# Weight casts of a fused attention and mixture-of-experts kernel moved to VectorE, and its attention weights staged through one buffer

## The chip, the cores and the metric

The kernel runs on the 8 cores of one Trainium2 chip. Each core computes two of the 16 sequences by itself; the cores exchange nothing. The time is that of the slowest core, in microseconds of device time. The trace is that of one profiled execution, on the slowest of its cores.

## The reference

```python
x = x + _layernorm(_attn(_layernorm(x), Wq, bq, Wk, bk, Wv, bv))   # out = einsum('bqk,bqd->bkd', softmax(q k / 32), v)
x = x + _layernorm(_ffn(_layernorm(x), gate_w, w1, w2, w3, ws1, ws2, ws3))

# _ffn, for all tokens t and experts e:
weights, indices = _gate(xt, gate_w)      # softmax over 16 experts, best 2 of 4 groups, best 4 experts
c = c.at[arange(T)[:, None], indices].add(weights)
h1 = einsum('td,edi->tei', xt, w1)
h3 = einsum('td,edi->tei', xt, w3)
y = einsum('tei,eid,te->td', silu(h1) * h3, w2, c)
z = silu(xt @ ws1) * (xt @ ws3) @ ws2
```

x is 16 sequences of 2048 tokens with 1024 features, all in float32. An expert's w1 and w3 are 1024x512, its w2 is 512x1024; ws1, ws2, ws3 are 1024x1024.

## The kernel before

A core works through its two sequences ("batches", b = 0 and 1) one after the other. Every expert is computed for every token, and its result is multiplied by the token's gate weight (zero for most). The shared expert is cut into two more of the same shape, so there are NPE = 18 units for each chunk of 512 tokens, four chunks (g = 0 to 3) a batch, and 72 units a batch.

The program is written by hand as five queues, one for each engine: "t" TensorE (PE in the profile), "v" VectorE (DVE), "s" ScalarE (ACT), "g" GpSimd (POOL) and "d" SyncE (SP), which issues all DMAs. `pr.on(engine, function)` appends a function to a queue, and each engine works through its queue in the order in which the functions were appended. `mark` and `wait` are semaphores between them. All engine instructions go through one helper, so the profile puts them on line 33, all DMAs on line 61 and the waits on line 57; they are told apart by tiles and shapes.

Each batch has these stages:

- *Attention weights* (lines 325 to 382). Wq, Wk, Wv come in two halves of 2 MB each (`h0`, `h1`), both issued at once into `wstA`, a part of the large buffer `RA`. DVE casts each half to bf16 into `Wbf` (128x4096 a cast), then PE transposes it and ACT copies the result to `RW`. The next weight's halves are issued after the cast of both, and its first cast waits for the transposes. Then PE spreads the bias row bv over the partitions, and ACT copies that to `bvrep` (lines 384 to 403).
- *Projections* (lines 405 to 516), from x loaded in tiles of 128 tokens (`a1_d`) and normalized by `emit_ln`, whose square root runs on ACT; then scores, softmax and the attention output, which leaves x1 in DRAM (`x1park`).
- *Router* (`back_kb`, `gate_group`) for the four tiles of a chunk: layernorm, transposes, the gate's logits, and a long row of small DVE operations that picks the experts.
- *Units* (lines 1143 to 1157). For unit u PE does h1(u) (32 matmuls of 128x512), y(u-1) (4 column groups `q_` of 8 matmuls) and h3(u) (32). ACT does four silu, DVE four multiplications `amul` of silu(h1) with h3 into `apb`, which y reads, and four accumulations `stt` of y into `Ysb`, which is `RA`. y uses two pairs of PSUM banks in turn: its third and fourth column groups wait for the first and second accumulation of the same unit (line 1014). The accumulations of unit u-1 stand on DVE ahead of the multiplications of unit u.
- *Final layernorm and output* (`fin_tile`), a chunk behind; POOL adds the residual (`outadd`), and SP sends the tile out. The last store of a batch waits on SP for POOL's addition.

In batch 0, chunk 0 (`conv` in `unit_dma`) the expert weights come as float32, in six pieces of 1 MB a unit (pieces 0 and 1: w1, 2 and 3: w3, 4 and 5: w2). They land in turn in the two halves of the staging buffer `wstF` (a part of `RV`); piece k+2 is sent when piece k has been cast. ACT casts pieces 0, 2, 3 and 4, POOL 1 and 5, into the unit's weight buffers. Two stores, `tee` (2 MB, after the casts of pieces 0 to 3) and `tee2` (1 MB, after 4 and 5), keep the bf16 weights in DRAM (`wbf16`), from which the other 126 units load them. The stores stand in SP's queue behind the unit's loads and ahead of the next unit's.

Of the kernel before, what the change touches and what calls it, by code (L numbers as in the profile page):

```python
# [12 lines left out]
P = 128  # L13
# [3 lines left out]
NEXP = 16  # L17
# [48 lines left out]
class Prog:  # L66
# [14 lines left out]
    def mget(self, key):  # L81
        return self.M.get(key)

    def mput(self, key, mark):
        self.M[key] = mark
# [22 lines left out]
def build(S, marks_in, stop=99):  # L108
    NB = 2
    TT = S // P  # L110
# [27 lines left out]
    with contextlib.ExitStack() as ctx:  # L138
# [15 lines left out]
        RA = ent(nc.sbuf_tensor("RA", [P, 16384], F32))  # L154
        RQ = ent(nc.sbuf_tensor("RQ", [P, 16384], BF16))
        RK = ent(nc.sbuf_tensor("RK", [P, 8192], F32))
        RV = ent(nc.sbuf_tensor("RV", [P, 8192], F32))
# [13 lines left out]
        pr = Prog(block, sems, dsems, marks_in)  # L171
        mget, mput = pr.mget, pr.mput
# [5 lines left out]

        RAb = RA[:].bitcast(BF16)
        Wbf = RAb[:, 0:8192]  # L180
        wstA = RA[:, 4096:12288]
        brow = RA[0:1, 12288:15360]
        gwsv = RA[0:NEXP, 15360:16384]
        xstage = RA[:, 4096:6144]
        xnbf = RAb[:, 12288:14336]
        sqA1 = RA[:, 7168:9216]
# [27 lines left out]
        def bankb(i, w=1):  # L214
            return PS[:, i * 512:(i + w) * 512].bitcast(BF16)
# [99 lines left out]
        try:  # L315
            for b in range(NB):
# [8 lines left out]
                for wi, (Wsrc, WTdst) in enumerate([(Wq, WTq), (Wk, WTk), (Wv, WTv)]):  # L325
                    key = f"b{b}w{wi}"

                    def a0_d(q, Wsrc=Wsrc, key=key, wi=wi, b=b):
                        if wi > 0:
                            q.wait(mget(f"b{b}w{wi - 1}cast"))  # L330
                        elif b > 0:
                            q.wait(mget(f"b{b - 1}ffn_cast_s"))
                            q.wait(mget(f"b{b - 1}ffn_cast_g"))
                        mput(key + "h0", q.dma(
                            wstA[:, 0:4096].rearrange("p (a d) -> p a d", a=4),
                            Wsrc[0:512, :].rearrange("(a p) d -> p a d", p=P),
                            pr.ds("wA")))
                        mput(key + "h1", q.dma(
                            wstA[:, 4096:8192].rearrange("p (a d) -> p a d", a=4),
                            Wsrc[512:1024, :].rearrange("(a p) d -> p a d", p=P),  # L340
                            pr.ds("wB")))
                    pr.on("d", a0_d)

                    def a0_v(v, key=key, wi=wi, b=b):
                        if wi > 0:
                            v.wait(mget(f"b{b}w{wi - 1}tr"))
                        elif b > 0:
                            v.wait(mget(f"b{b - 1}fin_done"))
                        v.wait(mget(key + "h0"))
                        v.tensor_copy(Wbf[:, 0:4096], wstA[:, 0:4096])  # L350
                        v.wait(mget(key + "h1"))
                        v.tensor_copy(Wbf[:, 4096:8192], wstA[:, 4096:8192])
                        mput(key + "cast", v.mark())
                    pr.on("v", a0_v)

                    def a0_t(t, key=key, wi=wi, b=b):
                        t.wait(mget(key + "cast"))
                        if b == 0 and wi == 0:
                            t.wait(mget("s_bias"))
                        if b > 0 and wi == 0:  # L360
                            t.wait(mget(f"b{b - 1}fin_done"))
                        for dt in range(DS):
                            pb = 6 + dt % 2
                            if dt >= 2:
                                t.wait(mget(key + f"tre{dt - 2}"))
                            elif wi > 0:
                                t.wait(mget(f"b{b}w{wi - 1}tre{dt + 6}"))
                            for a in range(DS):
                                t.transpose(bankb(pb)[:, a * P:(a + 1) * P],
                                            Wbf[:, a * 1024 + dt * P: a * 1024 + dt * P + P],  # L370
                                            identb[:])
                            mput(key + f"tr{dt}", t.mark())
                        mput(key + "tr", t.mark())
                    pr.on("t", a0_t)

                    def a0_s(s, key=key, WTdst=WTdst):
                        for dt in range(DS):
                            pb = 6 + dt % 2
                            s.wait(mget(key + f"tr{dt}"))
                            s.copy(WTdst[:, dt * 1024:(dt + 1) * 1024], bankb(pb)[:, 0:1024])  # L380
                            mput(key + f"tre{dt}", s.mark())
                    pr.on("s", a0_s)
# [22 lines left out]
                for cc in range(NCH):  # L405
                    gcc = b * NCH + cc

                    def a1_d(q, b=b, cc=cc, gcc=gcc):
                        if cc == 0:
                            q.wait(mget(f"b{b}w2cast"))  # L410
                        for ti in range(4):
                            gt = cc * 4 + ti
                            gti = b * TT + gt
                            q.wait(mget(f"T{gti - 2}ln"))
                            mput(f"T{gti}x",
                                 q.dma(xstage[:, (gti % 2) * D:(gti % 2 + 1) * D],
                                       x_in[b, gt * P:(gt + 1) * P, :],
                                       pr.ds("xA" if gti % 2 == 0 else "xB")))
                    pr.on("d", a1_d)

                    for ti in range(4):
# [503 lines left out]
                def cast_body(x, u, piece, b=b):  # L925
                    gslot = (u * 6 + piece) % 2
                    par = u % 2
                    x.wait(mget(f"b{b}U{u}p{piece}dma"))
                    if u >= 2:
                        x.wait(mget(f"T{u - 2}tee1" if piece < 4 else f"T{u - 2}tee2"))  # L930
                    if u >= 2:
                        if piece < 2:
                            x.wait(mget(f"b{b}U{u - 2}h1"))
                        elif piece < 4:
                            x.wait(mget(f"b{b}U{u - 2}h3"))
                        else:
                            x.wait(mget(f"b{b}U{u - 2}y3"))
                    else:
                        x.wait(mget(f"g{b * NCH + NCH - 1}qkvmm"))
                        if b > 0:  # L940
                            x.wait(mget(f"b{b - 1}ffn_mm_done"))
                    if piece < 2:
                        col, dstb = piece * 2048, wbufs[par]
                    elif piece < 4:
                        col, dstb = 4096 + (piece - 2) * 2048, wbufs[par]
                    else:
                        col, dstb = (piece - 4) * 2048, w2bufs[par]
                    if isinstance(x.e, bass.BassScalarEngine):
                        x.copy(dstb[:, col:col + 2048],
                               wstF[:, gslot * 2048:(gslot + 1) * 2048])  # L950
                    else:
                        x.tensor_copy(dstb[:, col:col + 2048],
                                      wstF[:, gslot * 2048:(gslot + 1) * 2048])
                    mput(f"b{b}U{u}p{piece}cast", x.mark())

                def unit_casts(u, b=b):
                    def uc_s(s, u=u):
                        for piece in (0, 2, 3, 4):
                            cast_body(s, u, piece)
                    pr.on("s", uc_s)  # L960

                    def uc_g(g_, u=u):
                        for piece in (1, 5):
                            cast_body(g_, u, piece)
                    pr.on("g", uc_g)

                def unit_h1(t, u, b=b):
                    g, e = u // NPE, u % NPE
# [165 lines left out]
                for g in range(NCH):  # L1134
# [8 lines left out]
                    for e in range(NPE):  # L1143
                        u = g * NPE + e
# [91 lines left out]
```

How the kernel before makes its waits and increments, by code:

```python
    def mark(self):  # L45
        if not self._marked:
            self._last.then_inc(self.sem, 1)
            self.n += 1
            self._marked = True
        return (self.sem, self.n)
# [1 line left out]
    def wait(self, mark):  # L52
        if mark is None:
            return
        sem, n = mark
        if n > 0:
            self.e.wait_ge(sem, n)
# [1 line left out]
    def dma(self, out, in_, s):  # L59
        sem, counts, key = s
        self.e.dma_start(out=out, in_=in_).then_inc(sem, 16)
        counts[key] += 16
        return (sem, counts[key])
# [1137 lines left out]
        def final_d(raw):  # L1201
            for k, n in finals.items():
                if n > 0:
                    raw.wait_ge(dsems[k], n)
```

## Time and profile before

| | |
|---|---|
| runs | 5165.06 us median of 3 (lowest 5155.02) |
| profiled execution | 5155.31 us, span 5153.7 us (core 1; the others 5138.4 to 5153.4) |
| granted clock, mean of the span | 0.881 to 0.884 on all cores |
| PE busy | 4145.2 us (80%) |
| DVE busy | 1956.8 us (38%) |
| ACT busy | 890.9 us (17%) |
| POOL busy | 154.7 us (3%) |
| DMA | 695.6 MB, mean 135 GB/s |

The busy shares are those of the whole span, over stages with different limits. PEclk is the granted clock as a share of 2.4 GHz. In the rows, `RV<-w` is a load of a float32 piece of an expert's weights, `wbf<-RW` a store of bf16 weights, `RW<-wbf` a load of them; a bracket gives the idle time of the engine before the group and what ended it.

### The profile page before, as it was taken

How to read it: one execution, taken by the hardware profiler on the slowest of the kernel's cores; microseconds unless marked ns; L12 is line 12 of the kernel's file. 1: busy time of each engine (PE TensorE's matmuls, PEld its weight loads, DVE VectorE, ACT ScalarE, POOL GpSimd, SP SyncE). 2: the span in 40 equal slices, each digit the busy share in tenths (PEclk: the TensorE clock that was granted, in tenths of full speed). 3: DMA queues.
4: the chain of work that ended last, by engine and by line, in shares of the span. 5: the costliest groups of instructions: out<-in, count | busy, mean ns of one | idle time of the engine just before them, and what ended most of it. 6: DMA issues, size and time to landing. Idle time of an engine off the chain costs nothing.

```text
span 5153.7 us, 53876 instructions; the slowest of 8 cores (5138.4 to 5153.7 us)
## 1 busy us (share of the span) xinstructions
PE 4145.2 (80%) x18864; PEld 1933.0 (38%) x18864; DVE 1956.8 (38%) x2996; ACT 890.9 (17%) x1350; POOL 154.7 (3%) x78
## 2 busy tenths in 40 slices
PE   4679757666899699879945679799979969996995
PEld 2234323222444344334423234344444434443442
DVE  2323532223433533443352333443343343344335
ACT  2124122222111111111102123111111111111110
POOL 0000001111000000000010000000000000000001
PEclk8789878888799799979976789899989979997997
DMA  3100478888344334334433101434334433433443
GB/s 123 33 9 13 137 234 277 275 275 266 131 157 153 108 138 153 120 130 159 150 101 120 33 9 37 159 123 150 128 123 156 149 121 138 149 119 128 154 153 108
DMA packets 123563, 695.61 MB, mean 135 GB/s; under 512 B 9620, under 2 KB 9620, under 8 KB 86440
## 3 DMA queue, kind: packets, MB, share of 16 engines
q1 hardware_dynamic: 123304, 692.18, 38.7%
q8 instruction: 160, 2.62, 0.2%
q14 instruction: 99, 0.81, 0.1%
HBM read 601.96 MB, written 90.18 MB: 134 GB/s over the span
## 4 chain that ended last, share of the span: by engine, by line
PE 67%; DMA 14%; DVE 9%; issue 4%; ACT 3%; POOL 2%; SPq 1%; DVEq 1%; POOLq 0%; ACTq 0%
PE PS L33 67%; DMA RV<-w 7%; DVE st L33 2%; DMA RK<-x 2%; DVE RK L33 2%; DVE RA L33 2%; DMA RV<-x1park 1%; POOL RW L33 1%; POOL RV L33 1%; DVE c_buf L33 1%; DVE glog L33 1%; DVE RV L33 1%; ACT RK L33 1%; ACT RW L33 1%; DMA RA<-Wv 1%
## 5 line engine op out<-in xcount | busy, mean ns | idle before, releaser
L33 PE MATMUL PS<-RQ,RW 128*128 128x512 bf16 x9216 | 2091.1, 389 | 275.7 <-POOL RW L33 183.9
L33 PEld LDWEIGHTS PS<-RQ,RW 128*128 128x128 bf16 x9216 | 917.9, 100 | 1424.8 <-issue 389.0
L33 PE MATMUL PS<-RW,RK 128*128 128x512 bf16 x4608 | 1036.4, 382 | 155.0 <-DVE RA L33 144.3
L33 DVE SCALAR_TENSOR_TENSOR RA<-PS,c_buf,RA 128x1024 f32<-128x1024 f32 x480 | 616.2, 1284 | 1319.2 <-PE PS L33 1318.7
L33 ACT ACTIVATE RK<-PS 128x512 f32<-128x512 f32 (+1 forms) x608 | 370.7, 620 | 2360.5 <-PE PS L33 2346.8
L33 PEld LDWEIGHTS PS<-RW,RK 128*128 128x128 bf16 x4608 | 433.8, 98 | 735.4 <-issue 265.6
L33 DVE TENSOR_TENSOR RK<-RK,PS 128x512 bf16<-128x512 f32 x576 | 394.0, 687 | 491.3 <-PE PS L33 491.1
L33 PE MATMUL PS<-identb,RA 128*128 128x128 bf16 x640 | 74.5, 295 | 309.8 <-DVE RA L33 299.0
L33 PE MATMUL PS<-RV,RA 128*128 128x512 bf16 x1024 | 228.4, 383 | 28.7 <-DVE RK L33 15.1
L33 PE MATMUL PS<-RA,RW 128*128 128x512 bf16 x1024 | 239.1, 398 | 8.5 <-DVE RA L33 8.5
L33 PE MATMUL PS<-RK,RQ 128*128 128x512 bf16 x1024 | 221.3, 379 | 3.0 <-DVE RV L33 3.0
L33 ACT CAST RW<-RV 128x2048 bf16<-128x2048 f32 x72 | 136.6, 1898 | 429.8 <-DMA RV<-w 367.2
L33 POOL TENSOR_TENSOR RV<-RV 128x1024 f32<-128x1024 f32 x32 | 85.3, 2667 | 3794.6 <-DMA RV<-x1park 2321.2
L33 PEld LDWEIGHTS PS<-identb,RA 128*128 128x128 bf16 x640 | 59.4, 133 | 328.5 <-issue 326.5
L33 PE MATMUL PS<-identf,RK 128*128 128x128 f32 x256 | 62.1, 424 | 138.1 <-DVE RK L33 138.1
L33 DVE TENSOR_TENSOR RV<-PS,RA 128x1024 bf16<-128x1024 f32 x32 | 39.2, 1224 | 323.2 <-PE PS L33 323.2
L33 PEld LDWEIGHTS PS<-RV,RA 128*128 128x128 bf16 x1024 | 99.1, 98 | 157.9 <-issue 45.6
L33 PEld LDWEIGHTS PS<-RA,RW 128*128 128x128 bf16 x1024 | 103.5, 102 | 142.3 <-issue 33.1
L33 PE MATMUL PS<-gwT,RK 128*128 128x16 f32 x512 | 114.2, 373 | 46.8 <-ACT RK L33 46.8
L33 PEld LDWEIGHTS PS<-RK,RQ 128*128 128x128 bf16 x1024 | 100.1, 98 | 124.2 <-issue 3.9
L33 PEld LDWEIGHTS PS<-gwT,RK 128*128 128x128 f32 x512 | 111.7, 331 | 58.7 <-issue 58.7
L33 ACT ACTIVATE st<-st 128x1 f32<-128x1 f32 x128 | 26.0, 203 | 621.3 <-DVE st L33 621.2
(73 smaller groups left out, 1597.7 us busy)
## 6 DMA issues: line engine op xcount, KB each, us to landing
RW<-wbf SPq DMA_DIRECT2D x126, 2048.0 KB, 7.8
RW<-wbf SPq DMA_DIRECT2D x126, 1024.0 KB, 4.8
RV<-w SPq DMA_DIRECT2D x96, 1024.0 KB, 7.6
wbf<-RW SPq DMA_DIRECT2D x18, 2048.0 KB, 14.6
wbf<-RW SPq DMA_DIRECT2D x18, 1024.0 KB, 7.7
RA<-x SPq DMA_DIRECT2D x32, 512.0 KB, 3.3
RK<-x SPq DMA_DIRECT2D x32, 512.0 KB, 4.5
x1park<-RK SPq DMA_DIRECT2D x32, 512.0 KB, 3.0
```

What stands on the lines that cost most here:

```text
L33: self._last = getattr(self.e, name)(*a, **k)
```

## The change

Three things are changed.

- The cast of pieces 1, 3 and 5 of each converted unit is done by DVE (before: piece 3 by ACT, 1 and 5 by POOL). `unit_casts(u)` is appended ahead of the accumulations of unit u-1 and the multiplications of unit u, so that is where the casts stand in DVE's queue.
- `wstA` becomes one buffer of 128x4096, the part of `RA` that holds tiles 12 to 15 of `Ysb`. Half 1 of a weight is issued after the cast of half 0. In batch 1, half 0 waits for the layernorm of the last tile in place of POOL's end. The bias rows and the router's weights move to `RV`.
- The x tiles of the first chunk no longer wait for the cast of Wv, in batch 1 for the layernorm of the last tile instead.

```diff
-        wstA = RA[:, 4096:12288]
-        brow = RA[0:1, 12288:15360]
-        gwsv = RA[0:NEXP, 15360:16384]
+        wstA = RA[:, 12288:16384]
+        brow = RV[0:1, 0:3072]
+        gwsv = RV[0:NEXP, 3072:4096]
...
                         elif b > 0:
                             q.wait(mget(f"b{b - 1}ffn_cast_s"))
-                            q.wait(mget(f"b{b - 1}ffn_cast_g"))
+                            q.wait(mget(f"b{b - 1}t{TT - 1}lny"))
                         mput(key + "h0", q.dma(
-                            wstA[:, 0:4096].rearrange("p (a d) -> p a d", a=4),
+                            wstA[:].rearrange("p (a d) -> p a d", a=4),
                             Wsrc[0:512, :].rearrange("(a p) d -> p a d", p=P),
                             pr.ds("wA")))
-                        mput(key + "h1", q.dma(
-                            wstA[:, 4096:8192].rearrange("p (a d) -> p a d", a=4),
-                            Wsrc[512:1024, :].rearrange("(a p) d -> p a d", p=P),
-                            pr.ds("wB")))
                     pr.on("d", a0_d)
...
                         v.wait(mget(key + "h0"))
-                        v.tensor_copy(Wbf[:, 0:4096], wstA[:, 0:4096])
+                        v.tensor_copy(Wbf[:, 0:4096], wstA[:])
+                        mput(key + "c0", v.mark())
+                    pr.on("v", a0_v)
+
+                    def a0_d1(q, Wsrc=Wsrc, key=key, b=b):
+                        q.wait(mget(key + "c0"))
+                        mput(key + "h1", q.dma(
+                            wstA[:].rearrange("p (a d) -> p a d", a=4),
+                            Wsrc[512:1024, :].rearrange("(a p) d -> p a d", p=P),
+                            pr.ds("wB")))
+                    pr.on("d", a0_d1)
+
+                    def a0_v1(v, key=key, b=b):
                         v.wait(mget(key + "h1"))
-                        v.tensor_copy(Wbf[:, 4096:8192], wstA[:, 4096:8192])
+                        v.tensor_copy(Wbf[:, 4096:8192], wstA[:])
                         mput(key + "cast", v.mark())
-                    pr.on("v", a0_v)
+                    pr.on("v", a0_v1)
...
                     def a1_d(q, b=b, cc=cc, gcc=gcc):
-                        if cc == 0:
-                            q.wait(mget(f"b{b}w2cast"))
+                        if cc == 0 and b > 0:
+                            q.wait(mget(f"b{b - 1}t{TT - 1}lny"))
...
                     def uc_s(s, u=u):
-                        for piece in (0, 2, 3, 4):
+                        for piece in (0, 2, 4):
                             cast_body(s, u, piece)
                     pr.on("s", uc_s)
 
-                    def uc_g(g_, u=u):
-                        for piece in (1, 5):
-                            cast_body(g_, u, piece)
-                    pr.on("g", uc_g)
+                    def uc_v(v, u=u):
+                        for piece in (1, 3, 5):
+                            cast_body(v, u, piece)
+                    pr.on("v", uc_v)
```

## Rows read from the trace of the kernel before

**Rows 1.** Windows: stretch, us, busy PE, PEld, DVE, ACT, POOL (count), PEclk, DMA share, GB/s.

```profile
665.00:1290.00 625.00, 418.79 (x1728) 174.78 (x1728) 161.41 (x230) 173.69 (x147) 66.26 (x35) 0.83 0.84 271
...
1352.00:1708.00 356.00, 355.50 (x1632) 157.73 (x1630) 134.68 (x139) 40.62 (x68) 0.00 (x0) 0.99 0.38 136
```

**Rows 2.** Waits of the DMA queue on SP, 665 to 1290: waited, times, longest.

```profile
SPq L57 <- ACT RW L33: 434.6, 72, 25.3
```

**Rows 3.** Timeline, staging casts and load issues of unit 9: start, us, what, idle before.

```profile
963.59 1.89 POOL L33 CAST RW<-RV 128x2048 bf16<-128x2048 f32 x1 [16.75 <-DMA RV<-w]
...
966.05 24.04 SPq L61 DMA_DIRECT2D RV<-w  x6
...
978.50 1.89 POOL L33 CAST RW<-RV 128x2048 bf16<-128x2048 f32 x1 [13.02 <-DMA RV<-w]
...
987.76 1.90 ACT L33 CAST RW<-RV 128x2048 bf16<-128x2048 f32 x1 [2.42 <-DMA RV<-w]
...
997.21 1.89 POOL L33 CAST RW<-RV 128x2048 bf16<-128x2048 f32 x1 [16.81 <-PE PS L33]
```

**Rows 4.** Timeline, h1 and h3 of that unit, an accumulation and the last multiplication.

```profile
980.65 9.42 PE L33 MATMUL PS<-RQ,RW 128*128 128x512 bf16 x32 [10.57 <-POOL RW L33]
...
991.97 1.28 DVE L33 SCALAR_TENSOR_TENSOR RA<-PS,c_buf,RA 128x1024 f32<-128x1024 f32 x1 [21.02 <-PE PS L33]
...
996.85 7.07 PE L33 MATMUL PS<-RQ,RW 128*128 128x512 bf16 x32
...
1004.10 0.69 DVE L33 TENSOR_TENSOR RK<-RK,PS 128x512 bf16<-128x512 f32 x1 [1.04 <-PE PS L33]
```

**Rows 5.** Groups by shape, DVE: busy us, mean ns of one, idle before.

```profile
L33 DVE CAST RA<-RA 128x4096 bf16<-128x4096 f32 x12 | 27.5, 2294 | 101.2 <-DMA RA<-Wq 47.2 <-DMA RA<-Wv 27.3 <-DMA RA<-Wk 16.6
...
L33 DVE TENSOR_SCALAR RA<-RA,st 128x1024 bf16<-128x1024 f32 x32 | 26.0, 812 | 5.5 <-DVE st L33 5.3
```

**Rows 6.** Timeline, unit 0: its last cast, and the gate's last operation.

```profile
683.77 1.89 POOL L33 CAST RW<-RV 128x2048 bf16<-128x2048 f32 x1 [30.83 <-DMA RV<-w]
...
689.38 0.22 DVE L33 TENSOR_TENSOR c_buf<-c_buf,smkb 128x64 f32<-128x64 f32 x1
```

**Rows 7.** Timeline, unit 17: its last cast, and its y.

```profile
1268.04 1.89 POOL L33 CAST RW<-RV 128x2048 bf16<-128x2048 f32 x1 [16.42 <-DMA RV<-ws]
...
1275.65 7.07 PE L33 MATMUL PS<-RW,RK 128*128 128x512 bf16 x32 [1.33 <-DVE RK L33]
```

**Rows 8.** Timeline, two idle times of PE in other stretches.

```profile
491.03 15.39 PE L33 MATMUL PS<-RV,RA 128*128 128x512 bf16 x64 [6.82 <-ACT RV L33]
...
1735.72 5.60 PE L33 MATMUL PS<-RW,RK 128*128 128x512 bf16 x16 [23.28 <-DVE RA L33]
```

**Rows 9.** Timeline, attention weights of the first batch, and tile 0's square root.

```profile
12.22 0.95 SPq L61 DMA_DIRECT2D RA<-Wq  x2
...
23.64 2.29 DVE L33 CAST RA<-RA 128x4096 bf16<-128x4096 f32 x1 [23.64 <-DMA RA<-Wq]
...
31.41 0.92 SPq L61 DMA_DIRECT2D RA<-Wk  x2
...
83.77 0.22 ACT L33 ACTIVATE st<-st 128x1 f32<-128x1 f32 x1
```

**Rows 10.** Timeline, attention weights of the second batch.

```profile
2702.34 1.15 SPq L61 DMA_DIRECT2D RA<-Wq  x2
...
2718.62 0.92 SPq L61 DMA_DIRECT2D RA<-Wk  x2
...
2728.56 2.29 DVE L33 CAST RA<-RA 128x4096 bf16<-128x4096 f32 x1 [10.01 <-PE PS L33]
...
2734.76 0.92 SPq L61 DMA_DIRECT2D RA<-Wv  x2
```

**Rows 11.** DMA issues of the page: count, KB each, median us to landing.

```profile
RW<-wbf SPq DMA_DIRECT2D x126, 2048.0 KB, 7.8
RW<-wbf SPq DMA_DIRECT2D x126, 1024.0 KB, 4.8
```

## The prediction

> **What bounds the kernel now.** I first cut the trace into stretches with the windows view. The expert units of the first batch's first token chunk, the only ones that convert weights, take 625 us for 18 units, or 34.7 us each, with the clock at 0.83 and the DMA engines 84% busy; the 18 units of the next chunk take 356 us at 0.99 [rows 1]. So this stretch is not bound by TensorE. The waits of SP's queue in it say by what: SP stands 434.6 us behind ACT's casts [rows 2].
>
> The timeline of one unit shows the cycle. Call T the end of the cast of a unit's last piece, p5 (for the unit shown first, 965.48). Only then does SP send the next unit's p0 and p1, since the store `tee2` ahead of them waits for that cast. The odd pieces, which share one half of the staging buffer, set the pace [rows 3]: p1's cast starts at T+13.0 (its transfer shares the engines with p0 and the two stores), takes 1.9; p3's starts 7.4 after that cast has ended, takes 1.9; p5's starts 7.5 after that (989.66 to 997.21), takes 1.9. Together 33.6 us. The mean cycle, from 685.66 to 1269.93 in 17 units, is 34.4 [rows 6, 7].
>
> TensorE runs h1, y of the unit before, and h3 in one go from T+15.2 to T+38.4, that is 4.8 us past the next T, and idles 10.6 us before it. 32 matmuls take 7.07 us in h3, but 9.42 us in h1 right after the idle time, 2.35 more: some eleven of them ran at the lower clock level, half the full one (11 x 0.22) [rows 4]. It has no claim on the ring: a unit's matmuls follow the casts, and no cast follows them closely.
>
> **The change, part by part.**
>
> *Casts on DVE instead of POOL and ACT.* Odd pieces go to DVE (ACT had p3, POOL p1 and p5). The cost of one: 128x4096 elements take 2.294 us and 128x1024, in a tensor_scalar with the same types, 0.812; on a straight line 2048 take 1.3. Bounds are half of 2.294, 1.15, and twice the 1.284 that a two-input pass over 1024 takes, 2.6; I take 1.3, as the line runs through the same operation [rows 4, 5]. The Trainium skill ("VectorE: DVE Perf Modes", the perf-mode tier table) states 1227 ns for such a float32 copy of 2048; by it 17 units would come out 3.6 us shorter in all. So three casts in the ring save 0.6 each, 1.8 a unit.
>
> *What stands in the same queue.* DVE now has, in this order: casts 1, 3, 5 of unit u; four accumulations of unit u-1; four multiplications of unit u; cast 1 of unit u+1. The queue holds its order: where DVE had other work ahead of an accumulation, y's second half waited 23.28 us [rows 8]. Now y(u-1) can do two of its four column groups, and then waits for the first accumulation, which stands behind cast 5, that is until T+1.28, with hand-over T+1.45. Then 16 matmuls of y and 32 of h3: 48 x 0.221 = 10.6 us at the full clock. TensorE will have idled: it starts h1 about T+16.7, needs 9.4 for it at worst and 3.5 for the half of y, and stands from T+29.6 to the next T+1.45 (T+35.6), some 6 us. After 6.82 us of idle time 64 matmuls took 15.39 instead of 14.0 [rows 8], so I expect the lower level again, and take unit 9's 2.35 us [rows 4]. h3 ends at T+14.4, the last multiplication 0.9 later (1003.92 to 1004.79) at T+15.3 [rows 4]. Only then comes cast 1, though its data landed at T+13.0.
>
> The ring: 15.3 + 1.3 + 7.4 + 1.3 + 7.5 + 1.3 = 34.1 against 33.6, or +0.5 in this unit. In a mean unit, 0.8 us longer, the excess costs nothing new if it lies in p1's landing (then -0.3), and stays if in the later legs (+0.5). I take +0.2: 17 x 0.2 = **+3.4 us**. What was won on three casts is given back by the wait for h3 and the multiplications.
>
> *First unit.* Cast 1 of unit 0 stands on DVE behind the gate, whose last operation ends at 689.60. POOL did it without waiting for the gate. Its end is 690.9, then p3 7.4 + 1.3 and p5 7.5 + 1.3, so T is 708.4 instead of 685.66 [rows 3, 6]: **+22.7 us**. Nothing gives that back, since the next unit's loads wait for T.
>
> *Last unit.* Before, y(17) starts 5.7 us after T (1269.93 to 1275.65). Now the multiplications end at T+15.3, y starts at T+15.5: **+9.8 us**, and the router of the next chunk follows it [rows 7].
>
> *The attention weights.* Two halves of 2 MB in flight become one staging buffer: load, cast 2.3, load, cast 2.3. What is a 2 MB load alone? 1 MB and 2 MB of bf16 weights land in 4.8 and 7.8 us, so 1.8 fixed and 3.0 a MB [rows 11]. In the first batch a pair took 16.8 (19.2 less the cast), alone 1.8 + 15.0/2 = 9.3; in the second 13.9 of 16.3, alone 7.9 [rows 9, 10]. First batch: 2 x 9.3 + 4.7 = 23.3 for 19.2, three times, **+12.3**. Second: first weight 20.5 for 16.3, +4.2; the second weight's first cast waits for the transposes of the one before, 9.9 after its issue as now, then 2.4 + 7.9 + 2.4 = 22.6 for 16.1, +6.5; the third I take between these, +5.3: **+16.0**. The lower bound is 7.8 a load throughout (the first batch then waits for transposes as well, about +1.2 a weight), together +20; the upper is the pair's rate unimproved, 11.4 for the half that landed first, together +45. The Trainium skill ("DMA: Bandwidth & Descriptors", anatomy of one DMA) gives 2.0 us plus bytes at 436 GB/s, 6.8 for 2 MB; by it this part would be about +13 instead of +28. The trace speaks against it: 2 MB took 7.8 even in longer runs of bytes per row [rows 11].
>
> *The x loads.* They go out before the last weight's second cast. That brings nothing: tile 0's square root on ACT starts at 83.77, behind the copies of the bias row, some 14 us after the last cast (12.22 + 3 x 19.2 = 69.8) [rows 9]; a landing and three short DVE passes fit in that. Without this cover the gain would be one landing of 0.5 MB, 1.8 + 1.5 = 3.3 us [rows 11], a batch. Beside the last half they cost between 0 and 3.0 us (1 MB at 3.0); half of it, twice: **+3.0**.
>
> *New waits at the second batch's start.* Load 0 waits for the last layernorm, not POOL's end. In SP's queue the last output store, which waits for POOL, stands ahead, so nothing is gained. Bias rows and router weights change only their place: nothing.
>
> Sum: 3.4 + 22.7 + 9.8 + 12.3 + 16.0 + 3.0 = 67.2. The profiled execution took 5155.3 (span 5153.7), 9.8 below the median of the runs and level with the lowest: 5155.3 + 67.2 = **5222 us**.
>
> **Rivals.**
>
> *A: TensorE keeps its full clock over the shorter idle time.* h3 ends 2.35 earlier, cast 1 starts at about T+13.1, the cycle is 31.9, -1.7 a unit, -29 in all; the last unit +7.5. Sum 22.7 - 29 + 7.5 + 31.3 = +32, 5188 us. For it: an idle time of 1.33 us leaves y at full pace [rows 7]. Against: the row with 6.82 us [rows 8].
>
> *B: the transfers shorten.* If p3 starts later, it finds the engines emptier, and 1 MB has landed in 4.8 where they were free [rows 11]. Half way to that, p3 and p5 are 1.2 to 1.3 shorter, -2.4 a unit, -41: 5181 us. Against it: the engines are 84% busy already, and p5 runs beside the store in both orders.
>
> *C: slower.* The chain cast 5, accumulation, y, h3, multiplications, cast 1 becomes the ring at the low clock. If idle gaps twice a unit keep TensorE at the lower level, 48 matmuls take 48 x 0.43 = 20.5 us, cast 1 starts at T+23.3, and the cycle is 42, +7.8 a unit, +133 in all, the last unit +17.8: 5360 us. It passes +103 us (2%) once cast 1 starts later than about T+17.7. For it: two gaps a unit where there was one, clock 0.83 already. Against: h3 went at full pace each time after 9.4 us of work.
>
> **How the numbers follow.** Forecast 0.62 (own range 5205 to 5245: loads alone make +20 to +45 of their +31, the unit's -0.3 to +0.5), A 0.12, B 0.12, C 0.14, of which 0.03 is a milder case that ends below 2%. A measurement of this kernel can tell about 2% from no change, 103 us. Faster by that means 170 us less than forecast, 0.01; slower, C, 0.11; the rest 0.88. The range that leaves out 2 in 10 reaches down to B and up past the bounds of the loads into the mild C: 5180 to 5275.
>
> **What would show it.** In the changed profile: cast 1 of unit 0 right behind the gate's last operation, T near 708; in each unit a break of TensorE inside y, released by DVE, then 11 or so slow matmuls; DVE casts of 1.3 us, the one of p1 right behind the fourth multiplication and not released by a DMA; mean cycle 34.6; weight loads 9.3 and 7.9 us. The forecast is wrong if p1's cast is released by its DMA (A), if p3 lands in under 6 us (B), or if the clock in the stretch falls well below 0.8 (C).

## The result and the profile after

| | before | after |
|---|---|---|
| runs | 5155.02, 5159.68, 5165.06 | 8, from 5206.08 to 5218.50, median 5213.6 |
| profiled execution | 5155.31, span 5153.7 | 5213.94, span 5212.4 (core 2) |
| spans of the 8 cores | 5138.4 to 5153.7 | 5183.7 to 5212.4 |

The ratio is 1.0101, 95% interval [1.0085, 1.0117]: 52 us slower. In some executions the four cores of one die or of both run at a lower clock, with any of these kernels, and these are left out of the times and ratios; the *core mean* below is the mean time of the cores of all dies that kept the clock of 0.88.

Windows of the changed kernel on core 2, the converting chunk and the chunk behind it (columns as in [rows 1]), then the waits of SP's queue in the first of them:

```profile
683.00:1327.00 644.00, 437.61 (x1728) 180.20 (x1728) 220.79 (x278) 138.75 (x128) 0.00 (x0) 0.84 0.82 263
...
1389.00:1745.00 356.00, 355.59 (x1631) 158.10 (x1632) 134.94 (x139) 40.63 (x68) 0.00 (x0) 0.99 0.38 136
```

```profile
SPq L57 <- ACT RW L33: 386.0, 52, 14.2
...
SPq L57 <- DVE RW L33: 158.4, 54, 23.0
```

POOL has no work left in the converting chunk, DVE has 220.8 us instead of 161.4, the clock stays at 0.84 and the next chunk is as it was. Groups by shape (busy us, mean ns of one, idle before) give the price of a cast, 1226 ns on DVE against 1898 on ACT:

```profile
L33 ACT CAST RW<-RV 128x2048 bf16<-128x2048 f32 x54 | 102.5, 1898 | 478.8 <-DMA RV<-w 356.7 <-PE PS L33 77.8 <-DMA RV<-ws 44.2
...
L33 DVE CAST RW<-RV 128x2048 bf16<-128x2048 f32 x54 | 66.2, 1226 | 282.1 <-DMA RV<-w 224.4 <-PE PS L33 36.4 <-DMA RV<-ws 21.1
```

Where the time came from is read by stage, from the start and end times that the timelines of all eight cores give (means over the cores, us; T is the end of a unit's p5 cast, the cycle is the way from T of unit 0 to T of unit 17, by 17):

| stage | before | after | difference | forecast |
|---|---|---|---|---|
| start to first projection | 107.7 | 121.3 | +13.6 | +13.8 |
| to the gate of chunk 0 | 521.7 | 524.4 | +2.7 | 0 |
| gate to T of unit 0 | 55.0 | 73.0 | +18.0 | +22.7 |
| cycle, a unit | 34.41 | 33.90 | 17 x -0.51 = -8.7 | +3.4 |
| T of unit 17 to the next chunk's gate | 24.6 | 33.5 | +8.9 | +9.8 |
| to batch 1's first weight load | 1403.1 | 1403.9 | +0.8 | 0 |
| to batch 1's first projection | 88.9 | 106.1 | +17.2 | +17.5 |
| to the end | 2361.8 | 2363.0 | +1.2 | 0 |

The differences add to +53.7. How far stages move without any change in them shows in a second execution of the kernel before (the last experiment): +0.5, +0.8, 0.0, 17 x -0.04, 0.0, +0.8, -0.3 and +4.5 us, +5.6 together. The weight stages, seen in the timeline (start, us, what, idle before) of batch 0 and then of batch 1:

```profile
22.25 2.29 DVE L33 CAST RA<-RA 128x4096 bf16<-128x4096 f32 x1 [22.25 <-DMA RA<-Wq]
...
35.35 2.29 DVE L33 CAST RA<-RA 128x4096 bf16<-128x4096 f32 x1 [10.80 <-DMA RA<-Wq]
...
101.19 0.22 ACT L33 ACTIVATE st<-st 128x1 f32<-128x1 f32 x1
```

```profile
2734.53 11.47 SPq L61 DMA_DIRECT2D RA<-Wq  x2
...
2755.46 13.08 SPq L61 DMA_DIRECT2D RA<-Wk  x2
...
2765.81 2.29 DVE L33 CAST RA<-RA 128x4096 bf16<-128x4096 f32 x1 [10.42 <-PE PS L33]
...
2778.19 12.26 SPq L61 DMA_DIRECT2D RA<-Wv  x2
```

The cast of Wq's second half starts 10.8 us after that of the first has ended: load and cast now follow each other. The first square root stands at 101.19, where [rows 9] have 83.77. In batch 1 it is about 21 us from the load of Wq to that of Wk and 23 from there to Wv; the first cast of Wk waits for the transposes, as forecast.

Unit 0: the gate's last operation, and the DVE casts of p1, p3 and p5.

```profile
704.03 0.22 DVE L33 TENSOR_TENSOR c_buf<-c_buf,smkb 128x64 f32<-128x64 f32 x1
704.20 1.23 DVE L33 CAST RW<-RV 128x2048 bf16<-128x2048 f32 x1
...
711.89 1.23 DVE L33 CAST RW<-RV 128x2048 bf16<-128x2048 f32 x1 [6.47 <-DMA RV<-w]
...
719.61 1.23 DVE L33 CAST RW<-RV 128x2048 bf16<-128x2048 f32 x1 [6.49 <-DMA RV<-w]
```

The first cast has no idle time before it and no releaser: its data lay there, and it stood behind the gate. T then comes 16.6 us after its start, since nothing can be sent before its buffer is free.

Unit 17: its last cast (T = 1298.26), the second half of y(16) behind it, and y(17).

```profile
1297.03 1.23 DVE L33 CAST RW<-RV 128x2048 bf16<-128x2048 f32 x1 [8.07 <-DMA RV<-ws]
...
1299.54 5.27 PE L33 MATMUL PS<-RW,RK 128*128 128x512 bf16 x16 [5.33 <-DVE RA L33]
...
1313.05 7.07 PE L33 MATMUL PS<-RW,RK 128*128 128x512 bf16 x32 [1.33 <-DVE RK L33]
```

y(17) starts at T+14.8, where [rows 7] have T+5.7: half of y(16), h3 and the last multiplications now stand between.

The steady ring, from p5 of unit 8 (T = 994.83) to p3 of unit 9:

```profile
993.60 1.23 DVE L33 CAST RW<-RV 128x2048 bf16<-128x2048 f32 x1 [8.55 <-DMA RV<-w]
994.74 2.47 DVE L33 SCALAR_TENSOR_TENSOR RA<-PS,c_buf,RA 128x1024 f32<-128x1024 f32 x2
...
996.17 5.07 PE L33 MATMUL PS<-RW,RK 128*128 128x512 bf16 x16 [8.32 <-DVE RA L33]
...
1001.07 7.07 PE L33 MATMUL PS<-RQ,RW 128*128 128x512 bf16 x32
...
1008.32 0.69 DVE L33 TENSOR_TENSOR RK<-RK,PS 128x512 bf16<-128x512 f32 x1 [1.04 <-PE PS L33]
1009.12 1.23 DVE L33 CAST RW<-RV 128x2048 bf16<-128x2048 f32 x1
...
1018.15 1.23 DVE L33 CAST RW<-RV 128x2048 bf16<-128x2048 f32 x1 [7.80 <-DMA RV<-w]
```

TensorE breaks off inside y for 8.32 us, until DVE's first accumulation, which stands behind p5's cast; the 16 matmuls then take 5.07 us instead of 3.5 (5.6 in the mean of 16 units and all cores), the lower clock level for part of them. h3 follows at full pace, and p1's cast (1009.12, T+14.3) comes right behind the fourth multiplication with no idle time: the chain of the forecast. The new idle time of TensorE costs it nothing.

### The profile page after: what moved, and what is told of

The parts are those of the page before. It is cut to its first block, busy times and chain, and to the rows that moved or that the text cites. A ratio compares the mean times of both kernels' runs of the same rounds, so it can differ in the third digit from the quotient of the medians.

```text
span 5212.4 us, 53881 instructions; the slowest of 8 cores (5183.7 to 5212.4 us)
## 1 busy us (share of the span) xinstructions
PE 4167.5 (80%) x18864; PEld 1938.0 (37%) x18864; DVE 2019.5 (39%) x3050; ACT 856.9 (16%) x1332; POOL 85.9 (2%) x42
## 4 chain that ended last, share of the span: by engine, by line
PE 69%; DMA 12%; DVE 11%; issue 4%; ACT 2%; POOL 1%; DVEq 1%; SPq 0%; ACTq 0%; POOLq 0%
PE PS L33 69%; DMA RV<-w 6%; DVE st L33 3%; DVE RA L33 2%; DVE RK L33 2%; DMA RV<-x1park 1%; DMA RK<-x 1%; DVE RW L33 1%; POOL RV L33 1%; DVE c_buf L33 1%; DVE glog L33 1%; ACT RK L33 1%; DVE RV L33 1%; DMA RA<-Wq 1%; DVEq L57 1%
## 5 line engine op out<-in xcount | busy, mean ns | idle before, releaser
L33 PE MATMUL PS<-RW,RK 128*128 128x512 bf16 x4608 | 1077.8, 392 | 276.3 <-DVE RA L33 265.6
L33 PE MATMUL PS<-RV,RA 128*128 128x512 bf16 x1024 | 228.3, 383 | 27.2 <-DVE RK L33 13.6
L33 ACT CAST RW<-RV 128x2048 bf16<-128x2048 f32 x54 | 102.5, 1898 | 478.8 <-DMA RV<-w 356.7
L33 DVE CAST RW<-RV 128x2048 bf16<-128x2048 f32 x54 | 66.2, 1226 | 282.1 <-DMA RV<-w 224.4
L33 PEld LDWEIGHTS PS<-RA,RW 128*128 128x128 bf16 x1024 | 103.6, 102 | 142.6 <-issue 33.7
## 6 DMA issues: line engine op xcount, KB each, us to landing
wbf<-RW SPq DMA_DIRECT2D x18, 2048.0 KB, 14.3
```

Source lines behind the costliest of these rows:

```text
L33: self._last = getattr(self.e, name)(*a, **k)
```

## The experiments

**The staging alone.** The changed kernel with the casts of before.

```diff
-                        for piece in (0, 2, 4):
+                        for piece in (0, 2, 3, 4):
...
-                        for piece in (1, 3, 5):
-                            cast_body(v, u, piece)
-                    pr.on("v", uc_v)
+                        for piece in (1, 5):
+                            cast_body(g_, u, piece)
+                    pr.on("g", uc_g)
```

> The kernel before with the new staging of the attention weights and x alone; the expert casts stay on ACT and POOL. Theory 1 (the loss is the serial loads plus the first and last converted unit): the first projection starts 13 to 17 us later, the second batch's weights take 17 to 18 us more, conversion stretch unchanged (cycle 34.4, y of unit 17 at T+5.7); +31 us, ratio 1.006. Theory 2 (the loss comes from DVE's queue in the conversion stretch, and the loads are mostly hidden): +5 to +10 us, ratio 1.001 to 1.002.

Measured: 5175.4, 5178.4, 5219.5 and 5236.3 us, where before on that chip took 5145 to 5155 and once 5176; the ratio, 1.0108 [1.0039, 1.0176], is too wide to use. The core mean is 5167 for 5141, +26. By stages: start to first projection 120.4 (+12.7), batch 1's weights 104.4 (+15.5). Together +28.2, where weights and x tiles were forecast at +31.3, both a little below the range expected here. But the cycle was 33.99, where two executions of before gave 34.41 and 34.37, though nothing in the loop differs.

**The casts alone.** The kernel before with the three odd casts on DVE.

```diff
-                        for piece in (0, 2, 3, 4):
+                        for piece in (0, 2, 4):
...
-                    def uc_g(g_, u=u):
-                        for piece in (1, 5):
-                            cast_body(g_, u, piece)
-                    pr.on("g", uc_g)
+                    def uc_v(v, u=u):
+                        for piece in (1, 3, 5):
+                            cast_body(v, u, piece)
+                    pr.on("v", uc_v)
```

> The kernel before with the casts of the odd pieces on DVE alone. Theory 1: unit 0's T is 19 us later, 17 cycles of 33.9 instead of 34.4 give back 8, y of unit 17 starts 9 later after T; +20 us, ratio 1.004. Theory 2: +42 to +47 us, ratio 1.0085.

Measured: 5172.6 to 5178.4 us, ratio 1.0037 [1.0016, 1.0059], core mean 5163 for 5141, so about +20, as expected. Gate to T of unit 0: 72.8 (+17.8). T of unit 17 to the next gate: 33.6 (+9.0). Cycle 33.71 (-0.7, or -12 in 17). So by the core means the two halves of the change make +26 and +21, 47 of the 52, and both ends of the row of units show what the whole change shows.

**Unit 0 as before.** The changed kernel, but unit 0 is cast by ACT and POOL.

```diff
                 def unit_casts(u, b=b):
+                    if u == 0:
+                        def uc0_s(s, u=u):
+                            for piece in (0, 2, 3, 4):
+                                cast_body(s, u, piece)
+                        pr.on("s", uc0_s)
+
+                        def uc0_g(g_, u=u):
+                            for piece in (1, 5):
+                                cast_body(g_, u, piece)
+                        pr.on("g", uc0_g)
+                        return
```

> The changed kernel with the six casts of unit 0 on ACT and POOL as before. Theory 1 (unit 0's cast 1 waits behind the gate on DVE, and nothing gives that back): T of unit 0 is 19 us earlier and so is everything behind it, ratio to before 1.0064. Rival (the later units absorb it, since they are paced by the DMA engines): under 5 us, ratio 1.009 to 1.010.

Measured: 5185.8, 5191.7 and 5199.7 us, ratio 1.0073 [1.0044, 1.0101] (expected 1.0064). Gate to T of unit 0 is 55.0 again, as in before. So the 18 us of that stage come from unit 0's casts on DVE, and the rows above show how: cast 1 stands behind the gate and the other two follow it. They are not won back later. The profiled execution's mean span is 5171.8, 29.6 below the changed kernel's, of which this stage is 18.0 and the cycle, 33.55, another 6, though no cast of the cycle was changed.

**The fifth cast behind the accumulations.** The changed kernel; y is no longer held up by p5's cast.

```diff
-                        for piece in (1, 3, 5):
+                        for piece in (1, 3):
...
                             unit_stt(u - 1)
+                        if b == 0 and g == 0:
+                            unit_cast5(u)
                         unit_sv(u)
```

> The changed kernel with one order swapped on DVE: the cast of piece 5 of unit u stands behind the accumulations of unit u-1 instead of ahead of them. Theory 1 (the accumulations stuck behind cast 5 hold back y, h3 and with them the next cast 1): TensorE's break inside y is gone, cast 1 starts when its data lands, T+13.7, cycle 32.4 to 32.9, y of unit 17 at T+6; 25 to 33 us less than the changed kernel, so ratio to before 1.004 to 1.005. Theory 3 (the ring is bound by the DMA engines, 82 to 84% busy, so an earlier cast only waits longer for its data): cycle stays at 33.9, only the last unit's 9 us come back, ratio 1.008.

Measured on cores 0 to 3: cycles 33.71 to 34.09, as in the changed kernel; T of unit 17 to the next gate 26.3 instead of 33.5; one run of 5202.5 us. By the cycle, that is the outcome expected for a ring bound by the transfers, but p5's leg speaks against so simple a reading. DVE's timeline on core 1, where p5's cast is the second row:

```profile
954.69 1.28 DVE L33 SCALAR_TENSOR_TENSOR RA<-PS,c_buf,RA 128x1024 f32<-128x1024 f32 x1 [0.44 <-PE PS L33]
955.89 1.22 DVE L33 CAST RW<-RV 128x2048 bf16<-128x2048 f32 x1
...
971.96 1.23 DVE L33 CAST RW<-RV 128x2048 bf16<-128x2048 f32 x1 [8.35 <-DMA RV<-w]
```

p1's cast is now released by its DMA, but p5's stands behind the accumulations, and its leg (from the end of p3's cast to its own start) has grown from 7.8 to 9.1 us, the mean of these four cores. The wait was moved, not removed. The test isn't clean, save for the last unit, where it shows that the +8.9 there are y waiting for DVE.

**The x tiles behind the last cast.** The changed kernel with the wait of before in `a1_d`.

```diff
-                        if cc == 0 and b > 0:
-                            q.wait(mget(f"b{b - 1}t{TT - 1}lny"))
+                        if cc == 0:
+                            q.wait(mget(f"b{b}w2cast"))
```

> The changed kernel with the x tiles of the first chunk waiting for the last weight's cast again. The forecast charged the early x loads 1.5 us a batch for sharing the engines with the last half of Wv: the load of that half would be 1.5 us shorter and the first projection start 1.5 us earlier (mean over the cores 119.8 instead of 121.3 us). If they cost nothing, no difference in the first projection's start.

Measured: 5204.5 us; start to first projection 119.6 instead of 121.3, batch 1's weights 105.0 instead of 106.1. That is 1.7 and 1.1 us less (forecast 1.5 each), but four kernels with the same program in these stages had 120.4 to 121.3 and 104.4 to 106.6: in batch 1 a cost of the early x tiles isn't shown, in batch 0 hardly. They gain nothing either. The loop is that of the changed kernel, and its cycle was 33.99.

**No wait for the multiplications, two ways.** The kernel before, with unit 0 as it was. In the first, POOL keeps p1 and DVE has p3 and p5:

```diff
-                        for piece in (0, 2, 3, 4):
+                        for piece in (0, 2, 4):
...
+                        cast_body(g_, u, 1)
...
+                    def uc_v(v, u=u):
+                        cast_body(v, u, 3)
+                        if u < NPE - 1:
+                            cast_body(v, u, 5)
```

> The kernel before (its staging, unit 0 as before), with the casts of pieces 3 and 5 on DVE from unit 1 on and piece 1 left on POOL (piece 5 of unit 17 too). Cast 1 no longer stands behind the multiplications. Theory 1 (the ring is a sum of transfers and casts; what DVE's queue adds to cast 1 is what the change gave back): 13.7 + 1.9 + 7.3 + 1.2 + 7.7 + 1.2 = 33.0 us a cycle, 23 us less than before in all, ratio 0.9955. Theory 3 (transfers stretch to fill what the casts leave, since the DMA engines are 84% busy): cycle 33.7 to 33.9 as in the runs with odd casts on DVE, 9 to 12 us less, ratio 0.998.

In the second DVE has all three, with cast 1 of the next unit between the accumulations and the multiplications:

```diff
                             unit_stt(u - 1)
+                        if b == 0 and g == 0 and 1 <= u < NPE - 1:
+                            unit_cast1(u + 1)
                         unit_sv(u)
```

> The kernel before (its staging, unit 0 as before), with all three odd casts on DVE from unit 1 on, and the cast of piece 1 of unit u+1 ahead of the multiplications of unit u, in place of behind them (piece 5 of unit 17 on POOL). Theory 1: cast 1 starts at its landing, 13.7 + 1.2 + 7.3 + 1.2 + 7.7 + 1.2 = 32.3 a cycle, 36 us less than before, ratio 0.993. Theory 3: cycle 33.7 to 33.9, 9 to 12 us less, ratio 0.998.

Measured: 5149.7 to 5155.9 us and 5146.5 to 5154.9 us. The core means are 5143 and 5139, for 5147 of before on that chip: 4 and 7 us less, under the 9 to 12 of the second theory and far under the 23 and 36 of the first. DVE's timeline in the second kernel (core 4), p5's cast of one unit and p1's of the next (here at T+15.2):

```profile
954.03 1.23 DVE L33 CAST RW<-RV 128x2048 bf16<-128x2048 f32 x1 [7.54 <-DMA RV<-w]
...
970.46 1.23 DVE L33 CAST RW<-RV 128x2048 bf16<-128x2048 f32 x1 [5.93 <-DMA RV<-w]
```

The legs of the ring, means over 8 cores and 17 units:

| kernel | p1's cast starts | p3's leg | p5's leg | three casts | cycle |
|---|---|---|---|---|---|
| before | T+13.8 | 7.35 | 7.59 | 5.7 | 34.4 |
| staging alone | T+13.6 | 7.16 | 7.56 | 5.7 | 34.0 |
| after | T+14.9 | 7.56 | 7.77 | 3.7 | 33.9 |
| after, x tiles behind the last cast | T+15.0 | 7.45 | 7.84 | 3.7 | 34.0 |
| casts alone | T+14.9 | 7.42 | 7.73 | 3.7 | 33.7 |
| p1 on POOL | T+14.5 | 7.30 | 7.90 | 4.4 | 34.0 |
| cast 1 ahead of the multiplications | T+14.4 | 7.81 | 7.90 | 3.7 | 33.8 |
| store behind two loads (below) | T+11.1 | 8.31 | 7.94 | 5.7 | 33.0 |
| both | T+12.0 | 8.30 | 8.12 | 3.7 | 32.2 |
| before, small stores (below) | T+10.1 | 7.33 | 6.64 | 5.7 | 29.8 |
| cast 1 ahead, small stores | T+10.4 | 7.50 | 7.10 | 3.7 | 28.7 |

With the wait gone, p1's cast is released by its DMA, but at T+14.4, 0.6 later than in before, and the legs behind it are 0.8 longer together: 0.6 of the 2.0 us is left. DVE's queue can't be the cause of that. The landings in the traces say where it lies: in both kernels SP sends p3 and p5 0.07 us after the cast that frees their buffer, and each of the three casts starts 0.2 to 0.3 us after its data has landed. What has grown is the time from issue to landing, in the mean from 12.5 to 13.0 us for p1, 7.1 to 7.5 for p3 and 7.3 to 7.6 for p5. p3 now goes out 2.1 us behind p2, where it went 2.8 behind; that the two share the engines for longer would lengthen it, but that is argued. In the changed kernel the same reading splits p1's 1.1 us: 0.4 is a later landing, 0.7 the wait behind the multiplications.

**Stores almost taken away.** To ask whether the transfers take the saving back, the two stores of each unit from the third on were cut to 512 columns, in before and in the kernel with cast 1 ahead. This leaves out part of the result: the later chunks load other units' weights.

```diff
-                            m1 = q.dma(wbufs[par], wbf16[e, :, 0:8192],
+                            m1 = q.dma(wbufs[par], wbf16[e % 2, :, 0:8192],
...
-                                 q.dma(wbf16[e, :, 0:8192], wbufs[par],
+                                 q.dma(wbf16[e, :, 0:(8192 if e < 2 else 512)], wbufs[par][:, 0:(8192 if e < 2 else 512)],
...
-                                 q.dma(wbf16[e, :, 8192:12288], w2bufs[par],
+                                 q.dma(wbf16[e, :, 8192:(12288 if e < 2 else 8704)], w2bufs[par][:, 0:(4096 if e < 2 else 512)],
```

> The kernel before, with the stores of the converted weights cut from 3 MB to 0.26 MB a unit from unit 2 on (the later units all load the weights of units 0 and 1, so this part of the result is left out). The ring asks for 6.6 MB a unit instead of 9.4. Theory 3 (bandwidth): cycle falls by 6 to 9 us, to 26 to 28. Theory 1 (a sum of waits in which the stores don't count): under 3 us.

> The same cut of the stores in the kernel with all odd casts on DVE and cast 1 ahead of the multiplications. Here the casts of the ring are 2.0 us shorter in sum (three of 1.23 for three of 1.90). Theory 3: with the engines freed, shorter casts count almost in full, cycle 1.3 to 2.0 below the one of the kernel before with small stores (with full stores it was 34.41 against 33.79, 0.6). Rival: they count no more than before, 0.6 or less, so that bandwidth was not what took the saving.

Measured: cycle 29.8 and 28.7, with 6.6 instead of 9.4 MB a unit. The first falls by 4.6, between what the two theories expected (6 to 9, under 3); the second is 1.1 below the first, again between (1.3 to 2.0, at most 0.6). Windows of before (core 1), of cast 1 ahead (core 4), and of these two (cores 4 and 2), 700 to 1100:

```profile
700.00:1100.00 400.00, 271.99 (x1126) 113.76 (x1127) 91.50 (x92) 112.72 (x95) 44.34 (x24) 0.84 0.86 274
```

```profile
700.00:1100.00 400.00, 278.59 (x1133) 116.71 (x1134) 129.86 (x128) 91.81 (x84) 0.00 (x0) 0.86 0.87 280
```

```profile
700.00:1100.00 400.00, 307.14 (x1258) 129.79 (x1284) 102.54 (x104) 129.83 (x107) 51.12 (x27) 0.88 0.69 227
```

```profile
700.00:1100.00 400.00, 315.34 (x1277) 134.22 (x1304) 150.92 (x148) 106.53 (x98) 0.00 (x0) 0.88 0.73 234
```

The engines go from 0.86 busy to 0.69, and of the 4.6 us 3.7 lie in p1's start. The short casts are worth 1.1 us there (29.8 to 28.7) where they are worth 0.6 with the full stores. If that difference is real, contention with the stores accounts for 0.5 of the 1.4 us that are lost; but 0.5 is little more than the 0.4 by which kernels with the same loop differ. The other 0.9 lie again between issue and landing (+0.3 for p1, +0.2 for p3, +0.5 for p5), though a quarter of the engines' time is idle. Why these transfers are longer isn't shown.

**The store behind two loads.** Before, with `tee2` of the unit before issued after pieces 0 and 1 of the next.

```diff
                             for piece in range(6):
+                                if piece == 2 and u > 0:
+                                    tee2_body(q, u - 1)
...
-                        pr.on("d", tee2)
+                        if u == NPE - 1:
+                            pr.on("d", tee2)
```

> The kernel before with one order changed on SP: the 1 MB store of unit u-1 is issued behind the loads of pieces 0 and 1 of unit u, no longer ahead of them, so that p0 goes out when piece 4 has been cast, some 5 us before T. Theory 1 (the ring is paced by when it may ask): p1 lands 2 to 3 us earlier after T, cycle 31.5 to 32.5, 32 to 49 us less, ratio 0.991 to 0.994. Theory 3 (paced by the engines' bandwidth): the transfers of p3 and p5 take longer by what p1 wins, cycle 33.9 or more, under 10 us less, ratio above 0.998.

Measured: 5129.7 to 5151.3 us, core mean 5125 for 5147 of before on that chip, cycle 33.0, -1.4, between the two theories. p1's cast starts 2.7 us earlier in the cycle, and p3's and p5's legs take 1.3 of it back. So the order of the store was a real cost, about half of what it looked like. The edit does two things at once: the store no longer runs ahead of p1, and p0 goes out at T-4.3 in place of T+0.6, since it no longer waits behind the store for p5's cast. Which of them counts isn't shown.

**Before again, and both orders together.** The first is the kernel before, unchanged; the second is before with cast 1 ahead of the multiplications and the store behind two loads.

> The kernel before, unchanged, for a second trace of it: how far do the stages move between two executions? If the trace of before is typical, the mean cycle over the cores is 34.3 to 34.5 us, and the 0.4 to 0.7 by which the kernels with DVE casts stay below it are real. If it is 34.0, as in the kernel with the new staging alone, they are within what executions differ by.

> The kernel before (its staging, unit 0 as before) with odd casts on DVE from unit 1 on, cast 1 ahead of the multiplications, piece 5 of unit 17 on POOL, and the store tee2 behind the loads of pieces 0 and 1. Store order alone gave cycle 33.0, cast order alone 33.8. If both add up: 32.4, 34 us less than before, ratio 0.993. If the engines' bandwidth is the floor: 32.8 to 33.0, 24 to 27 us less, ratio 0.995.

Measured: before took 5168.1 us in its profiled run, 5157.3 to 5170.1 in others, cycle 34.37. By the rule written down for it the lower cycles would be real; but the staging alone, with the same loop, had 33.99, so the rule was too simple. Both orders together took 5114.1, 5118.3 and 5122.3 us, ratio 0.9911 [0.9893, 0.9929], cycle 32.2. Its window, on core 3:

```profile
700.00:1100.00 400.00, 282.46 (x1167) 118.85 (x1166) 132.32 (x132) 91.83 (x84) 0.00 (x0) 0.85 0.90 287
```

The engines are 0.90 busy (0.89 to 0.91 over the cores), the most of any kernel here. This version is 46 us faster than before and some 95 faster than the change. -2.2 a unit is the sum of the two edits (-0.6 and -1.4) within the scatter.

## Why the prediction was right and wrong

*The time.* 5222 was forecast and 5214 measured, +67 against +52, inside the range. Slower was right in its sign. Part of the nearness is luck: the cycle was forecast 12 us too high and the first unit 4.7, and +4.7 in stages forecast at nothing took some of that back.

*The step that failed: the chances.* The prediction set 0.88 on no change that could be told, on the ground that "A measurement of this kernel can tell about 2% from no change". The interval of this comparison is 0.16% to either side, and those of the part changes are 0.2 to 0.7%. A forecast of +1.3% was therefore a forecast of slower, and the chances should have said so. The prediction had the numbers for it: two of its three times lay 10 us apart, and the five terms of its sum that don't come from the cycle made +63.8, six times that. In the sum the step that failed is the cycle, below: "I take +0.2", where the runs showed -0.5.

*Attention weights and x: right.* +30.8 measured, +31.3 forecast. From issue to landing the loads that had no x tile beside them took 9.1 us in the mean of all cores in batch 0 (forecast 9.3; 7.5 to 10.6) and 8.2 in batch 1 (forecast 7.9; 7.4 to 10.4). The x tiles' +3.0 is not shown, as said above. The estimate from the Trainium skill ("DMA: Bandwidth & Descriptors", anatomy of one DMA), 6.8 a load, is below every one of them; the page fits it to DMAs issued from GpSimd, and these are issued from SyncE.

*First unit: right in its place, 4.7 too large.* Two terms were mis-sized. The legs behind the late cast: I took 7.4 and 7.5 from the steady ring, and they were 6.47 and 6.49 in the rows of unit 0, which has no unit before it whose stores could run beside them (that this is the reason wasn't tried); with 1.23 for a cast, T came 16.6 behind the gate's end, not 18.8, which is 2.2 of the 4.7. And the gate itself: from its first logits matmul (`PS<-gwT,RK`) to its last DVE operation it took 57.7 to 58.1 us on all cores before and 56.3 on all cores after, 1.6 less (the reason stands in the last section). The remaining 0.9 is that in the execution I read the chain from, T of unit 0 lay 54.15 behind the gate's start on its core, where the mean is 55.0.

*Last unit: right,* +8.9 for +9.8.

*Cycle: wrong in sign, by 0.7 us a unit, 12 us in all.* The absolute ring was good, 34.1 forecast and 33.9 measured, in part because three errors of its terms, told further down, partly cancel. What it was compared with was not. The step reads "In a mean unit, 0.8 us longer, the excess costs nothing new if it lies in p1's landing (then -0.3), and stays if in the later legs (+0.5). I take +0.2". The table of legs settles it: over 17 units and 8 cores p1's cast starts at T+13.8 (13.0 in unit 9) and the two legs make 14.94 (14.9). The excess lies in p1's landing, all of it; -0.3 was the right end, and it could have been read from the trace of before. That is 0.5 of the 0.7. Then p1's cast came at T+14.9, not T+15.3 (-0.4), the casts took 1.23, not 1.3 (-0.2), and the legs grew by 0.4 (+0.4). The Trainium skill ("VectorE: DVE Perf Modes", the perf-mode tier table) has 1227 ns for such a cast; the trace agrees, with 1226. How much of the -0.5 the change of engine made is not sharp: with ACT's and POOL's casts the cycle was 34.41, 34.37 and 33.99 in three executions, with DVE's 33.99, 33.90, 33.71 and 33.55. The means differ by 0.47, and kernels with the same loop by up to 0.4.

*"What was won on three casts is given back by the wait for h3 and the multiplications"* is half the truth. The wait is there, 0.7 us a unit behind p1's landing, but without it most of the saving is lost as well, to p1 landing later and longer legs.

*The rivals.* A fell: y's half after the break ran low, and p1's cast stood behind the multiplications, at T+14.9, not T+13.1. But that half started at T+1.35 and took 5.6 us in the mean, 2.1 more than 3.5, not 2.35 more; these two make most of the 0.4 by which p1's cast came earlier. B fell: the legs got longer, not shorter. C fell: the clock stayed at 0.84, and the fourteen h3 on core 2 between 740 and 1220 all took 7.07. What none of them holds is the +4.7 in three stages forecast at nothing, +2.7 of it ahead of the gate; in the kernel with the staging alone that stage shows +0.7, with the x tiles behind the last cast +0.7, with unit 0 as before +2.2, and in before again +0.8, so I take it for scatter, which isn't proven.

## What to carry to other kernels

Work that is given to a faster engine also takes a place in its queue: here the price was paid at the two ends, +18 us where the first cast stood behind the gate and +9 where the last unit's y stood behind casts, against 7 to 15 us less in the 17 cycles between (four kernels), of which 7 also came in a kernel whose loop was not touched. In a ring of loads and casts whose DMA engines are 0.86 busy, 2.0 us of shorter casts were worth 0.6, and the order in which a store stands among the loads 1.4. Read the legs of a ring as means over all its rounds, not from one round with a guess at the rest; and judge a small forecast by the scatter of the runs, not by a round figure.

## What the runs showed of the hardware

- POOL's cast held up a DVE operation. DVE's timeline in the gate, before (core 1), while POOL casts p5 of unit 0 from 683.77 to 685.66 [rows 6], and the same operations after (core 2):

```profile
683.92 1.76 DVE L33 TENSOR_TENSOR glog<-smkb 128x12 f32<-128x12 f32 x1
685.79 0.17 DVE L33 TENSOR_TENSOR c_buf<-c_buf,glog 128x12 f32<-128x12 f32 x1
```

```profile
700.17 0.17 DVE L33 TENSOR_TENSOR glog<-smkb 128x12 f32<-128x12 f32 x1
700.44 0.17 DVE L33 TENSOR_TENSOR c_buf<-c_buf,glog 128x12 f32<-128x12 f32 x1
```

  An operation of 0.17 us took 1.76 and ended as POOL's cast ended; all other operations of the gate are equal to 0.02 us. On all cores, the ten executions with POOL's casts in unit 0 have a gate of 57.7 to 58.2 us, the four without 56.2 to 56.4. The Trainium skill ("SBUF — State Buffer", two separate sides) states that a DVE operation with two SBUF inputs and a GpSimd one that reads SBUF exclude each other for their whole length; the trace agrees. The prediction had missed this, a gain of 1.6 us.

- Two idle times of the same length were followed by different paces. In the changed kernel, h1 (32 matmuls) took 7.07 us after 2.25 and 8.64 after 2.25:

```profile
1214.95 7.07 PE L33 MATMUL PS<-RQ,RW 128*128 128x512 bf16 x32 [2.25 <-DVE RW L33]
...
1248.51 8.64 PE L33 MATMUL PS<-RQ,RW 128*128 128x512 bf16 x32 [2.25 <-DVE RW L33]
```

  The 8.64 are the lower clock level for part of the matmuls. The length of the last break alone doesn't set the level.
- A 2 MB float32 load with no x tile or second load of its core beside it took 7.5 to 10.6 us at batch 0's start (on core 4 7.9 in the mean, on core 2 10.4) and 7.4 to 10.4 at batch 1's, in one execution of the changed kernel; [rows 11] have 7.8 for 2 MB of bf16. What makes the difference was not tested.
- Executions with the same loop, instruction for instruction, had cycles up to 0.4 us apart in the means over eight cores (34.41, 34.37, 33.99; and 33.99, 33.90, 33.71, 33.55). What sets this wasn't found.
